# A GNN and FFN kernel on one core: first turns of the count blocks sized one to four chunks by a table

## The reference

```python
def _sage_layer(h, edge_src, edge_dst, deg_inv, W_self, W_neigh, b):
    msg = h[edge_src]
    agg = jax.ops.segment_sum(msg, edge_dst, num_segments=h.shape[0])
    mean = agg * deg_inv[:, None]
    return h @ W_self + mean @ W_neigh + b
...
    h = jax.nn.relu(_sage_layer(x, edge_src, edge_dst, deg_inv, W_self0, W_neigh0, b0))
    out = _sage_layer(h, edge_src, edge_dst, deg_inv, W_self1, W_neigh1, b1)
...
    x = x + _L0_gnn_ref(_layernorm(x, axis=-1), src, dst, ...)
    x = x + _L0_ffn_ref(_layernorm(x, axis=-1)[None], L0_ffn_W_fc, L0_ffn_W_proj)[0]
```

## Time and profile before

| | us |
|---|---|
| time before, median of 3 runs (1589.86 to 1591.72) | 1590.83 |
| the profiled execution's own time | 1590.69 |
| its span, first to last instruction | 1588.0 |
| PE busy | 1576.3 |
| DVE busy | 875.7 |
| ACT busy | 461.7 |
| POOL busy | 139.4 |
| matmuls of L1557 (446 of them), busy | 56.0 |
| stretch in which the count steps lie | 57 to 279 |

### The profile page before, as it was taken

One profiled execution on the slowest core, in us unless ns is written; L12 is line 12 of the kernel. 1 busy time (PEld: TensorE's weight loads), 2 busy tenths in 40 slices (PEclk: granted clock), 3 DMA queues, 4 the chain that ended last, 5 costly groups with the idle time before them and its releaser, 6 DMA issues.

```text
span 1588.0 us, 23284 instructions
## 1 busy us (share of the span) xinstructions
PE 1576.3 (99%) x7764; PEld 1335.2 (84%) x7764; DVE 875.7 (55%) x1645; ACT 461.7 (29%) x855; POOL 139.4 (9%) x278
## 2 busy tenths in 40 slices
PE   8999999999999999999999999999999999999998
PEld 7777777888888888889989899898998888888886
DVE  8777776464014124564434334343343788888868
ACT  3356665121012001122313123131231233333256
POOL 1351477000000000010000000000001000000000
PEclk9999999999999999999999999999999999999999
DMA  8323344675335545576202022021122333333222
GB/s 305 132 97 126 117 162 161 233 291 208 115 106 178 190 172 183 174 230 237 80 27 106 30 76 79 26 106 33 73 79 106 106 119 119 119 119 119 96 90 51
DMA packets 55978, 205.47 MB, mean 129 GB/s; under 512 B 5392, under 2 KB 14110, under 8 KB 50372
## 3 DMA queue, kind: packets, MB, share of 16 engines
q1 hardware_dynamic: 53204, 190.71, 33.9%
q0 software_dynamic: 2688, 13.63, 2.5%
HBM read 153.85 MB, written 51.52 MB: 129 GB/s over the span
## 4 chain that ended last, share of the span: by engine, by line
PE 96%; DVE 2%; issue 1%; DMA 1%; ACT 0%; SPq 0%; DVEq 0%; ACTq 0%
PE bank L1625 27%; PE bank L1758 27%; PE bank L1777 25%; PE bank L1707 11%; PE bank L1557 2%; PE bank L1599 2%; PE bank L1815 1%; DVE lif_a L1518 0%; DVE w L1254 0%; DMA w_raw<-w_neigh 0%; DVE lif_b L1518 0%; DMA pr_raw<-w_proj 0%; DVE y L1498 0%; DVE lif_c L1511 0%; DVE xt L1242 0%
## 5 line engine op out<-in xcount | busy, mean ns | idle before, releaser
L1625 PE MATMUL bank<-w,xt 128*128 128x512 f32 x1920 | 467.1, 396 | 0.6 <-DVE xt L1242 0.6
L1758 PE MATMUL bank<-x2t,fc_w 128*128 128x384 f32 (+1 forms) x2304 | 438.4, 350 | 0.8 <-ACT relu L1015 0.8
L1758 PEld LDWEIGHTS bank<-x2t,fc_w 128*128 128x128 f32 x2304 | 411.7, 188 | 26.0 <-issue 1.1
L1625 PEld LDWEIGHTS bank<-w,xt 128*128 128x128 f32 x1920 | 351.9, 188 | 69.5 <-DVE xt L1242 0.8
L1777 PE MATMUL bank<-pr_w,hid 128*128 128x512 f32 (+1 forms) x1728 | 394.8, 389 | 0.0
L1777 PEld LDWEIGHTS bank<-pr_w,hid 128*128 128x128 f32 (+1 forms) x1728 | 320.7, 186 | 70.8
L1468 DVE TENSOR_TENSOR y<-y,bank 128x512 f32<-128x512 f32 (+1 forms) x144 | 98.8, 687 | 206.9 <-PE bank L1777 206.9
L1010 ACT ACTIVATE pr_w<-pr_raw 128x1024 fp32r<-128x1024 f32 x64 | 67.1, 1049 | 366.3 <-PE bank L1777 362.9
L1707 PE MATMUL bank<-z,at 128*128 128x512 f32 x720 | 168.4, 392 | 0.0
L1707 PEld LDWEIGHTS bank<-z,at 128*128 128x128 f32 x720 | 133.9, 188 | 27.3
L1411 DVE TENSOR_TENSOR square<-relu 128x384 f32<-128x384 f32 (+1 forms) x96 | 56.9, 593 | 144.1 <-ACT relu L1015 144.1
(11 more groups left out here) (156 smaller groups left out, 1064.8 us busy)
## 6 DMA issues: line engine op xcount, KB each, us to landing
fc_raw<-w_fc SPq DMA_DIRECT2D x64, 512.0 KB, 4.2
pr_raw<-w_proj SPq DMA_DIRECT2D x64, 512.0 KB, 3.5
xt<-xt_dram SPq DMA_DIRECT2D x24, 1024.0 KB, 5.0
xt_dram<-xt SPq DMA_DIRECT2D x18, 1024.0 KB, 4.3
at<-at_dram SPq DMA_DIRECT2D x18, 640.0 KB, 5.5
part_dram<-rows SPq DMA_DIRECT2D x20, 512.0 KB, 3.9
rows<-part_dram SPq DMA_DIRECT2D x20, 512.0 KB, 4.2
rows<-x SPq DMA_DIRECT2D x17, 512.0 KB, 5.2
```

The source lines that it names most:

```text
L1625: ins = nc.tensor.matmul(bank[:, 2 * (u % 2) + q, :], xt[j][:, a, k, :], w[:, k, b, q * HALF:(q + 1) * HALF], start=(k == 0 and m == 0), s ...
L1758: ins = nc.tensor.matmul(bank[:, 4 + (c if g == 0 else j % 2), 0:n], fc_w[:, j % 2, k, a, :], x2t[g][:, k, v, c0:c0 + n], start=(k == 0 an ...
```

## The change

The chunks of a block's first turn come from a table with one digit for each window, `TURN_CHUNKS`, one to four; the further turns stay at four. A turn's chunks are split between the two sets, the first set taking the odd one: (1, 0), (1, 1), (2, 1) or (2, 2). With (1, 0) the second set is not visited: PE and DVE skip it, and ACT has no loop in that step. As sets are no longer visited equally often, DVE and PE count visits in one register for each set; each visited set's register goes up in every turn, where before the side's one register did. The loop's step is the sum of the two.

```diff
--- before.py
+++ after.py
@@ -77,7 +77,8 @@
 EXTRA_TURNS = dict(enumerate((8, 3, 2, 1, 1, 1, 1, 1, 1, 1))) | {12: 1}
 
 
-SHORT_TURNS = {1, 6, 7, 8, 9, 12, 24} | set(range(27, 80)) - {37}
+TURN_CHUNKS = ("4234432112441434433333332332222222222321"
+               "2122212212121211212112111211111111111111")
 
 
 def window_of(i):
@@ -97,7 +98,8 @@
 
 def chunks_of_set(i, j):
 
-    return 1 if j == 0 and window_of(i) in SHORT_TURNS else LOOP_SET
+    count = int(TURN_CHUNKS[window_of(i)]) if j == 0 else LOOP_CHUNKS
+    return ((count + 1) // 2, count // 2)
 
 
 TURNS = [(i, j) for i in range(WINDOWS) for j in range(extra_turns(i) + 1)]
@@ -878,16 +880,18 @@
 
             def src_one_hots(i, j):
 
-                count = chunks_of_set(i, j)
+                before, count = chunks_of_set(i, j)
                 side = side_of(i, j)
                 act_set, side_visit = LOOP_SETS[side][1], side_visits[side]
                 first, end = turns_of_step(act, registers, edge, i, j)
                 if (i, j) == OWN_STEPS[0]:
                     act.wait_ge(w_low, w_lows(1, 1))
-                with act.Fori(first, end, 2 * count) as g:
+                if count == 0:
+                    return
+                with act.Fori(first, end, before + count) as g:
                     act.wait_ge(act_hot_ready, visit)
                     for c in range(count):
-                        chunk = g + (count + c)
+                        chunk = g + (before + c)
                         ins = nc.scalar.activation(dist[:, c, :], iota[0:P, 0:128], ACT.Square,
                                                    bias=edge_col[:, 0, ds(chunk, 1)], scale=-1.0)
                     ins.then_inc(dist_ready, 1)
@@ -1164,9 +1168,9 @@
                 nc.vector.tensor_scalar(many_int[:, 0:1], many[:, 0:1], SAFE_GROUPS, None, ALU.is_gt).then_inc(many_ready, 1)
                 nc.vector.tensor_scalar(many_int[:, 1:2], many[:, 0:1], SAFE_GROUPS, None, ALU.is_le).then_inc(many_ready, 1)
 
-            side_visits = [dve.alloc_register(f"dve_visit{side}") for side in range(2)]
-            for side_visit in side_visits:
-                dve.reg_mov(side_visit, 1)
+            set_visits = {s: dve.alloc_register(f"dve_visit{s}") for own in LOOP_SETS for s in own}
+            for set_visit in set_visits.values():
+                dve.reg_mov(set_visit, 1)
             registers = range_registers(dve, "dve")
 
             edge = dve.alloc_register("dve_edge")
@@ -1181,24 +1185,25 @@
                         ins = nc.vector.tensor_scalar(key_of(s, c), iota[0:P, :], float(v * WINDOW_COLS),
                                                       current[:, side, 1, c:c + 1], ALU.add, ALU.is_equal)
                     ins.then_inc(key_hot_ready[s], 1)
-                count = chunks_of_set(i, j)
+                counts = chunks_of_set(i, j)
                 side = side_of(i, j)
-                visit = side_visits[side]
                 first, end = turns_of_step(dve, registers, edge, i, j)
                 if (i, j) == OWN_STEPS[0]:
                     dve.wait_ge(w_low, w_lows(1, 1))
-                with dve.Fori(first, end, 2 * count) as g:
+                with dve.Fori(first, end, sum(counts)) as g:
                     for place, s in enumerate(LOOP_SETS[side]):
-                        dve.wait_ge(hot_used[s], visit)
-                        for c in range(count):
-                            chunk = g + (count * place + c)
+                        if counts[place] == 0:
+                            continue
+                        dve.wait_ge(hot_used[s], set_visits[s])
+                        for c in range(counts[place]):
+                            chunk = g + (counts[0] * place + c)
                             if place == 0:
                                 nc.vector.tensor_scalar(src_of(s, c), iota[0:P, 0:128],
                                                         edge_col[:, 0, ds(chunk, 1)], None, ALU.is_equal)
                             ins = nc.vector.tensor_scalar(key_of(s, c), iota[0:P, :], float(v * WINDOW_COLS),
                                                           edge_col[:, 1, ds(chunk, 1)], ALU.add, ALU.is_equal)
                         ins.then_inc(key_hot_ready[s], 1)
-                    dve.reg_add(visit, visit, 1)
+                        dve.reg_add(set_visits[s], set_visits[s], 1)
 
             def layer_norm(l, n, source, target):
                 i, j = turned(l, n), n % 2
@@ -1545,9 +1550,9 @@
 
             for s in range(SETS):
                 pe.sem_inc(hot_used[s], 1)
-            side_visits = [pe.alloc_register(f"pe_visit{side}") for side in range(2)]
-            for side_visit in side_visits:
-                pe.reg_mov(side_visit, 1)
+            set_visits = {s: pe.alloc_register(f"pe_visit{s}") for own in LOOP_SETS for s in own}
+            for set_visit in set_visits.values():
+                pe.reg_mov(set_visit, 1)
             next_visit = pe.alloc_register("pe_next_visit")
             pe.reg_mov(next_visit, 2)
             registers = range_registers(pe, "pe")
@@ -1557,17 +1562,19 @@
                 return nc.tensor.matmul(bank[:, 4 + i % 2, 0:WINDOW_COLS], src_of(s, c), key_of(s, c),
                                         start=start, stop=stop)
 
-            def turn_of_edges(i, side, count, stop=False):
-                visit = side_visits[side]
+            def turn_of_edges(i, side, counts, stop=False):
                 for place, s in enumerate(LOOP_SETS[side]):
+                    if counts[place] == 0:
+                        continue
                     if place == 1:
                         pe.wait_ge(act_hot_ready, next_visit)
-                    pe.wait_ge(key_hot_ready[s], visit)
-                    for c in range(count):
-                        ins = product_of_chunk(i, s, c, stop=(stop and place == 1 and c == count - 1))
+                    pe.wait_ge(key_hot_ready[s], set_visits[s])
+                    for c in range(counts[place]):
+                        ins = product_of_chunk(i, s, c, stop=(stop and place == 1 and c == counts[1] - 1))
                     ins.then_inc(hot_used[s], 1)
-                pe.reg_add(visit, visit, 1)
-                pe.reg_add(next_visit, next_visit, 1)
+                    pe.reg_add(set_visits[s], set_visits[s], 1)
+                    if place == 1:
+                        pe.reg_add(next_visit, next_visit, 1)
 
             def step_of_edges(i, j):
                 last, head = extra_turns(i), HEAD_SETS[i % 2]
@@ -1581,10 +1588,10 @@
                         ins = product_of_chunk(i, head, c, start=(c == 0))
                     if not kept:
                         ins.then_inc(hot_used[head], 1)
-                count = chunks_of_set(i, j)
+                counts = chunks_of_set(i, j)
                 first, end = turns_of_step(pe, registers, edge, i, j)
-                with pe.Fori(first, end, 2 * count):
-                    turn_of_edges(i, side_of(i, j), count, stop=(j == last > 0))
+                with pe.Fori(first, end, sum(counts)):
+                    turn_of_edges(i, side_of(i, j), counts, stop=(j == last > 0))
                 if last == 0:
                     product_of_chunk(i, head, HEAD_CHUNKS - 1, stop=True).then_inc(hot_used[head], 1)
 
```

## The result

| | before | after |
|---|---|---|
| median of 22 runs, us | 1590.80 | 1588.63 |
| lowest and highest | 1589.47, 1591.89 | 1587.67, 1589.87 |
| profiled execution, its own time and span | 1590.69, 1588.0 | 1588.72, 1586.6 |

The ratio is 0.9987, 95% interval 0.9981 to 0.9993: 2.2 us faster, which is less than the 0.2% line and inside the forecast range. The direction and the mechanism held; the size was over-forecast, 3.08 us against 2.2, and its interval (1.1 to 3.0) leaves the 3.08 just out.

What follows compares the result with a forecast made beforehand. PE's own work was taken to bound the kernel: 44 chunk products fewer at 0.070 us give -3.08 us, all other parts 0, so 1587.7 us, ratio 0.998. The range was 1586.5 to 1589.6 us.

Steps and rivals of the forecast that it cites:

- D: Rival: the late last head product becomes the rule in PE's count steps, 26 us slower, 1614 us; chance 3%.
- the forecast's own range: The forecast's time was to lie from 1586.9 to 1588.7 us, 0.5 us either way from late steps; chance 74%.
- part (2): Register and wait instructions on PE: hidden by its sequencer, taken as nothing, bounds 0.53 us gain to 2.8 us loss.
- part (5): POOL, unchanged, must keep pace with shorter steps in S0; two heads are made ahead, so taken as 0.
- Rival B: POOL becomes the bound in the last 24 blocks, costing 2.2 us, 1589.9 us; chance 4%.
- A: Rival: PE's added register instructions show and eat the gain, up to 2.8 us, 1590.5 or 1589 us; chance 8%.
- C: Rival: the 0.53 us of late count steps on PE vanish too, 1587.2 us; chance 10%.

Runs made afterwards that it cites:

- e3: The changed kernel with four chunks in every first turn, 118 products more than the kernel before; ratio 1.0059 to the kernel before.
- e4: The changed kernel with four more register additions written per PE turn, which left one more register instruction in each of 101 turns; ratio 0.9988 to the kernel before.
- before, and again: The kernel before, unchanged, run once more for a second profile; that execution took 1590.51 us.
- e2: The changed kernel with the old chunk counts (2 or 4) in its table, both sets always visited, 446 chunk products; ratio 1.0006 to the kernel before.
- after, and again: The changed kernel, unaltered, run once more for a second profile; that execution took 1589.34 us.
- e8: The changed kernel with PE loading the ranges in odd blocks too, 80 loads in place of 40; ratio 0.9987 to the kernel before.
- e11: The changed kernel with PE's one load of four range registers made of four loads of one register each; ratio 1.0172 to the kernel before.
- e7: The changed kernel, PE loading four blocks' ranges at once in blocks 42, 50, 58, 66, 72, none in 44, 52, 60, 68, 74; ratio 0.9977, median 1586.88 us.
- e12: The changed kernel with only the 512 KB part store held back in S0's row tiles 5 to 9 until four count blocks are copied; ratio 0.9979.
- e9: The changed kernel with row-tile load and part store held back in S0's tiles 2 to 8 until four count blocks are copied; ratio 1.0068.

## Why the prediction was right, and where it was mis-sized

**Right.** 44 products fewer at 0.07 us (402 of them, slope 0.07 after and 0.071 in e3), all on the path. The 101 late first weight loads stayed (106 waits by issue after, as the late steps have some more). ACT and DVE gave nothing. No wait was added in A0: its twenty shortened steps take 0.17 or 0.18 us. The first step of S0 stayed late (0.32 before, 0.44 after). D did not come: of 101 steps three were late by more than 0.1 us beside that one.

**Not as forecast.** The first product of G0 was to come 3.1 us earlier. It came at 279.14 in place of 279.99 in the first pair of profiles, 0.85 earlier, and at 279.22 in place of 281.01 in the second, 1.79. That is where the loss shows. The time still lies in the forecast's own range, but just inside it (1588.63 against its end of 1588.7), and that owes something to luck: the range allowed 0.5 us for the late steps, and they cost 1.2.

**Mis-sized: part (2), "I take nothing".** I had seen the four late steps, put them down to PE's sequencer, and bounded their price by the smallest seen over the added additions, up to 2.8 us. The size of what came (1.2 us in the mean of two profiles) lies inside that bound, but not by that mechanism. "Their durations are not in the trace" was wrong: the rows above have them. An added addition takes 0.036 us, 2.5 us in all 70, close to the bound; it is hidden, and one more of that size doesn't show either (e4). I had named the register loads among what the sequencer hides. They take 0.33 us in most blocks, but 1.12 and 1.25 in blocks 52 and 68 before, and I hadn't noticed that blocks 52, 60, 68 and 74, the late ones, are all even, and so the ones with the load. That the sequencer works ahead was right; how far was not asked. The load starts 0.99 to 1.48 us before the step in the late blocks.

**What grew, and POOL, part (5), taken at 0.** In block 44 the load stands behind POOL's head, and it got longer. It also lost some cover, as POOL's pace didn't shorten with the steps:

| | load starts behind the store's issue, us | load takes | load starts ahead of the step | step late |
|---|---|---|---|---|
| block 44 before, and again | 0.90, 0.91 | 0.35, 0.33 | 1.28, 1.27 | 0, 0 |
| block 44 with six products, e2 and e3 | 0.62, 0.90 | 0.33, 0.33 | 1.18, 1.27 | 0, 0 |
| block 44 after, and again | 1.15, 1.16 | 1.59, 1.10 | 0.99, 0.99 | 0.98, 0.53 |
| block 52 before, and again | 1.15, 1.16 | 1.12, 1.52 | 1.17, 1.18 | 0.26, 0.65 |
| block 52 after, and again | 1.15, 1.15 | 1.25, 1.29 | 1.13, 1.13 | 0.60, 0.57 |
| block 52 in e3 | 0.67 | 0.33 | 1.39 | 0 |

The 0.29 us of cover alone would not have made block 44 late: a load of 0.35 fits into 0.99. What made it late is that the load became 0.8 to 1.2 us longer. With the same registers and six products (e2, e3) it is on time, with five it is late in all of after, after again, e4 and e8. The shorter steps moved the load from 0.90 to 1.15 us behind the store's issue; in the rows of blocks 44 and 52 all loads at 1.15 are long and all at 0.62 to 0.91 are short. That this shift is the reason is argued from these rows, no run moves it alone, and it is no general rule: block 74's load, 0.90 behind its store, takes 0.91. In block 68 the load stayed (1.25 before, 1.23 after) and the cover shrank, from 1.48 to 1.27. Rival B was wrong as priced, as no wait names POOL, and right in that POOL's head holds PE's sequencer back in these blocks.

**A**, the gain eaten by PE's sequencer, came nearest: part of the gain was lost in the sequencer, and late steps of four show it, but by the load and not by the added additions. **C**, the late steps vanish, came out the other way: they grew.

## What to carry to other kernels

Before costing register and loop instructions at nothing, ask for their own rows by line, since the timeline doesn't show them, and take the longest as well as the median (0.33 and 1.59 us here). Then ask how far ahead the sequencer can get: it starts from the last wait that it had to pass, here a one-hot made 1.1 us before, not from the start of the dense stretch. When a filler between matmuls is shortened, its own path through the other engines isn't, and instructions shift against transfers. And when a few steps are late without a releaser, list what they share (parity, a load, a store issued a microsecond before) ahead of giving them an average price.

## What the runs showed of the hardware

A register load from SBUF on PE's queue takes 0.33 us of the sequencer's time in a quiet stretch for four registers, 0.30 for one (e11) and 0.59 for eight (e7). DVE, ACT and POOL load the same four in 0.34, 0.31 and 0.32 us in the median, and up to 0.82, 1.03 and 1.23. When a 512 KB store from SBUF has been issued about 1 us before, PE's load can take up to 1.59 us, and the next product comes 0.15 us behind its end (block 44, after). That it is the store is shown (e12): with the store moved, the loads of the five blocks take 0.33 us. The load of a row tile need not run beside it: block 74 has none, and its load takes 0.89 us after (late by 0.04 to 0.28 in the profiles with the store in place, on time in e9). Why the store slows the load, and why a load at the same distance is slow in one block and not in another, stays open.

The Trainium skill (Advanced Engine Details and Errata, Control Flow Timing) gives 51 ns for a branch and 108 ns for a compare and branch. The trace doesn't agree with the second: the 101 COMPARE_BRANCH rows after have a median of 67 ns (64 before). With one in every step, hidden in nearly all of them, they are small beside the load.
